# GpSimd's copy in place of a casting transfer for the high half of an expert's weights

## What is computed

```python
logits = einsum('ed,btd->bte', gate_w, x)
scores = sigmoid(logits) + gate_b
weights, indices = top_k(scores, 4)
weights = weights / weights.sum(-1, keepdims=True)
shared_out = silu(x @ w1_shared) * (x @ w3_shared) @ w2_shared
h1 = einsum('btd,edc->btec', x, w1_routed)      # 16 x 512 x 352
h2 = einsum('btd,edc->btec', x, w3_routed)
h3 = silu(h1 * h2)
experts_out = einsum('btec,ecd->bted', h3, w2_routed)
routed_out = einsum('bted,bte->btd', experts_out, router_probs)
```

## Time and profile before

| | |
|---|---|
| Median of three runs | 990.17 us |
| The profiled execution | 990.58 us, of it 989.0 us span |
| Mean granted TensorE clock | 0.908 of full speed |
| Busy: TensorE, its weight loads | 817.7 us (83%), 694.2 us (70%) |
| Busy: VectorE, ScalarE, GpSimd | 425.3, 297.1, 493.6 us |
| GpSimd's queue: software DMA | 108.74 MB, 40.3% of the DMA engines' time |

### The profile page before, as it was taken

The page is one execution under the profiler, slowest core; times in us unless marked ns, Lnnn a source line. Parts: engine busy times, 40 slices in busy tenths (PEclk is TensorE's granted clock), DMA queues, the critical chain, the costliest instruction groups (busy, mean ns, idle before and its releaser), DMA issues.

```text
span 989.0 us, 16683 instructions
## 1 busy us (share of the span) xinstructions
PE 817.7 (83%) x4484; PEld 694.2 (70%) x4485; DVE 425.3 (43%) x864; ACT 297.1 (30%) x577; POOL 493.6 (50%) x357
## 2 busy tenths in 40 slices
PE   3647658786685787999999999999789999969992
PEld 3334536664573666988988888989679988768881
DVE  5576673674444456333333333333223333323331
ACT  1527246245323211222222223222122222212220
POOL 2853217323817645205066555065681168688772
PEclk9668767986987999999999999999889999989997
DMA  6683725806214425537279887497884588959999
GB/s 238 205 302 117 277 64 182 321 21 251 103 32 146 176 110 185 169 91 239 69 245 268 251 248 249 122 273 238 247 273 153 144 248 237 253 128 210 219 175 261
DMA packets 89258, 191.43 MB, mean 194 GB/s; under 512 B 7536, under 2 KB 26992, under 8 KB 89232
## 3 DMA queue, kind: packets, MB, share of 16 engines
q0 software_dynamic: 44800, 108.74, 40.3%
q1 hardware_dynamic: 33920, 61.13, 18.7%
q10 hardware_dynamic: 10512, 21.23, 5.8%
HBM read 85.43 MB, written 67.76 MB: 155 GB/s over the span
## 4 chain that ended last, share of the span: by engine, by line
PE 60%; POOL 11%; DVE 10%; ACT 7%; issue 7%; ACTq 2%; DMA 0%; DVEq 0%; POOLq 0%; SPq 0%
PE bank L594 33%; PE bank L611 14%; PE bank L602 3%; POOL acc L564 2%; PE bank L831 2%; POOL dispatched L508 2%; PE bank L698 2%; PE bank L716 2%; POOL ring_lo L431 2%; ACTq L1057 1%; DVE xr_lo L1419 1%; PE bank L739 1%; POOL hid L489 1%; POOL wa L480 1%; ACT xr_hi L887 1%
## 5 line engine op out<-in xcount | busy, mean ns | idle before, releaser
L594 PE MATMUL bank<-ring_hi,xr_hi 128*128 x632 | 170.1, 351 | 31.9 <-DVE xr_lo L1419 31.6
L594 PE MATMUL bank<-ring_lo,xr_hi 128*128 x632 | 155.5, 328 | 0.0
L594 PE MATMUL bank<-ring_hi,xr_lo 128*128 x632 | 155.4, 327 | 0.0
L594 PEld LDWEIGHTS bank<-ring_hi,xr_hi 128*128 128x128 f32 x632 | 107.0, 192 | 57.4 <-issue 57.3
L431 POOL TENSOR_TENSOR ring_lo<-raw,ring_hi 128x1408 fp32r<-128x1408 f32 x34 | 109.2, 3211 | 59.5 <-DMA ring_hi<-raw 59.2
L887 ACT ACTIVATE ht_hi<-bank 128x384 fp32r<-128x384 f32 x95 | 46.7, 492 | 270.0 <-PE bank L602 270.0
L611 PE MATMUL bank<-ring_hi,ht_hi 112*128 (+3 forms) x285 | 121.7, 427 | 5.8 <-DVE acc L1212 4.5
L1428 DVE TENSOR_TENSOR ht_lo<-bank,ht_hi 128x384 fp32r<-128x384 f32 x79 | 44.0, 557 | 177.6 <-ACT ht_hi L887 177.6
L611 PE MATMUL bank<-ring_lo,ht_hi 112*128 (+3 forms) x285 | 113.3, 398 | 0.0
L594 PEld LDWEIGHTS bank<-ring_hi,xr_lo 128*128 128x128 f32 x632 | 113.0, 191 | 0.0
L594 PEld LDWEIGHTS bank<-ring_lo,xr_hi 128*128 128x128 f32 x632 | 113.0, 191 | 0.0
(11 more groups left out here) (183 smaller groups left out, 1329.5 us busy)
## 6 DMA issues: line engine op xcount, KB each, us to landing
ring_hi<-raw POOLq DMA_DIRECT2D x34, 704.0 KB, 6.0
raw<-in_L_ffn_w_routed_dram POOLq DMA_DIRECT2D x32, 704.0 KB, 6.1
x_in<-dispatched SPq DMA_DIRECT2D x79, 264.0 KB, 4.0
expert_out<-zero_rows ACTq DMA_DIRECT2D x9, 2304.0 KB, 13.5
expert_out<-y_out SPq DMA_DIRECT2D x79, 256.0 KB, 4.3
ring_hi<-raw POOLq DMA_DIRECT2D x17, 768.0 KB, 4.5
raw<-in_L_ffn_w_routed_dram POOLq DMA_DIRECT2D x16, 448.0 KB, 4.6
dispatched<-zero_rows SPq DMA_DIRECT2D x1, 4224.0 KB, 15.9
```

Of the source, the lines that this page charges most:

```text
L594: last = mm(outs[m], half[:, c * P:(c + 1) * P], ring13(w, slot_at, c, m), start=(c == 0 and half is x_hi and w is ring13_hi), stop=(c == ...
```

## The change

`fill` no longer issues transfers for the high halves. GpSimd copies the raw weights into the `float32r` tile itself (`tensor_copy`), waits for its own copy, subtracts, and loads the next raw part at once; then the other weight in the same way, then W2. The semaphores `hi1_in`, `hi3_in`, `hi2_in`, which counted 16 for a transfer, become `hi1`, `hi3`, `hi2`, which count 1 for an instruction. `split_hidden` goes. The wait `free2` now stands behind W3's subtraction. Nothing else is changed.

```diff
-            "raw1_in raw3_in raw2_in hi1_in hi3_in hi2_in ready1 ready3 ready2 "
+            "raw1_in raw3_in raw2_in hi1 hi3 hi2 ready1 ready3 ready2 "
...
-            def split_hidden(n, slot, m):
-
-                hi, lo = (ring[:, slot * W13:(slot + 1) * W13].rearrange(
-                    "p (c m h) -> p c m h", c=KC, m=2)[:, :, m, :]
-                    for ring in (ring13_hi, ring13_lo))
-                pool.wait_ge(s[("hi1_in", "hi3_in")[m]], 16 * n + 16)
-                g.tensor_tensor(lo, raw13[:, :, m, :], hi.bitcast(F32),
-                                ALU.subtract).then_inc(s[("ready1", "ready3")[m]], 1)
-
...
                 free13()
                 wait_alone()
                 for m in range(2):
+                    hi, lo = (ring[:, slot * W13:(slot + 1) * W13].rearrange(
+                        "p (c m h) -> p c m h", c=KC, m=2)[:, :, m, :]
+                        for ring in (ring13_hi, ring13_lo))
+                    rounded, ready = (("hi1", "ready1"), ("hi3", "ready3"))[m]
                     pool.wait_ge(s[("raw1_in", "raw3_in")[m]], 16 * n + 16)
                     wait_alone()
-                    pool.dma_start(ring13_hi[:, slot * W13:(slot + 1) * W13].rearrange(
-                        "p (c m h) -> p c m h", c=KC, m=2)[:, :, m, :],
-                        raw13[:, :, m, :]).then_inc(s[("hi1_in", "hi3_in")[m]], 16)
-                split_hidden(n, slot, 0)
+                    g.tensor_copy(hi, raw13[:, :, m, :]).then_inc(s[rounded], 1)
+                    pool.wait_ge(s[rounded], n + 1)
+                    g.tensor_tensor(lo, raw13[:, :, m, :], hi.bitcast(F32),
+                                    ALU.subtract).then_inc(s[ready], 1)
+                    pool.wait_ge(s[ready], n + 1)
+                    wait_alone()
+                    load_next((1, 3)[m])
                 pool.wait_ge(s["raw2_in"], 32 * n + 32)
                 free2()
                 wait_alone()
-                pool.dma_start(ring2_hi[:, at2:at2 + W2], raw_2).then_inc(s["hi2_in"], 16)
-                split_hidden(n, slot, 1)
-                pool.wait_ge(s["ready1"], n + 1)
-                wait_alone()
-                load_next(1)
-                pool.wait_ge(s["ready3"], n + 1)
-                wait_alone()
-                load_next(3)
-                pool.wait_ge(s["hi2_in"], 16 * n + 16)
+                g.tensor_copy(ring2_hi[:, at2:at2 + W2], raw_2).then_inc(s["hi2"], 1)
+                pool.wait_ge(s["hi2"], n + 1)
```

## The result

| | before | after |
|---|---|---|
| Median (four runs each, 986.36 to 993.12 and 972.52 to 976.69) | 989.76 us | 974.5 us |
| The profiled execution, and its span | 990.58, 989.0 us | 972.52, 969.9 us |
| TensorE's waits for the tokens' low halves | 31.6 us in 26 | 16.2 us in 15 |
| GpSimd busy | 493.6 us | 531.0 us |
| GpSimd's queue: software DMA | 108.74 MB, 40.3% | 70.86 MB, 27.9% |

The ratio is 0.9846 (95% interval 0.9807 to 0.9886): 15.3 us faster, where 984 (977 to 992) was forecast. The direction and the places were right, the size was not: some two and a half times the gain came.

The account below looks back on a forecast made before the run. It took TensorE as the bound, stalled late by GpSimd's fills 11, 12 and 16. Terms −7.5 (these fills), +2.3 (fill 0), −0.9 (fill 2) and −0.4 (DMA relief) made −6.5, hence 984 us, range 977 to 992.

Parts of the forecast that it names:

- The copy and the fill: On GpSimd a copy takes 1.40 us for 1,408 elements, 1.50 for 1,536, and a whole fill 19.26 us.
- Fills 11 and 12: Two late weight fills behind TensorE's stalls at 701 and 721 us: 2.4 us gained over both.
- so it moves with TensorE, to 824.6: The gathers before fill 16 start on a store's landing that follows TensorE, so 824.6 for 827.00; 7.5 us gained altogether.
- So no clock loss is spared: At the last stall, fill 16 still misses ScalarE's wish by 4.1 us, and slower matmuls still follow the idle time.
- Most of the 22 small waits fall late, beside gathers, and stay; I take −0.4: TensorE's small waits, some 10 us together, gain only 0.4 us from 51 fewer transfers, with −4 as the end.
- Fill 2: Near 385 us, VectorE's cast ends sooner, −0.9 us; +3.7 if it meets GpSimd's second subtraction, −3.3 if everything slips between.
- Fill 0: In the first stretch, GpSimd's first subtraction holds up VectorE's small `q_scale` until 34.6 us: +2.3 us on the chain.
- Each microsecond on the copy costs 8: Each us on a copy costs 8 us: five at fill 12, two more at fill 16, one at fill 0.
- Rival 3: Faster: fill 2's cast comes free, small waits shorten, fill 0's delay is absorbed: near 977.5 us, chance 0.20.
- Rival 2: A copy as long as the subtraction, 3.2 us, makes fills 11, 12 and 16 later: 1006 us, chance 0.08.
- rival 1: First form: a copy of 2.1 us; second: 1.4 us with fill 2's cast caught: 990 us either way, chance 0.26.
- Rival 4: TensorE never waits for the transfers, so replacing them by copies changes nothing: 990 us, chance 0.04.

Follow-up runs that it names:

- the square of medians: Kernel before and changed kernel, each with register loads late (989.76, 974.5 us) or moved ahead of a wait (974.3, 965.55 us).
- experiment 4: Changed kernel with fill 0 alone done by transfers, as before: 972.07 us, ratio 0.9806 to the kernel before.
- Experiment 5: Changed kernel with each copy made twice, one behind the other: 1006.93 us, ratio 1.0170 to the kernel before.
- experiment 1: Changed kernel plus casting transfers of the old sizes between dead tiles beside fills 3 to 16: 996.48 us, ratio 1.0066 to the kernel before.

## Why the prediction was wrong, step by step

**The copy and the fill: right.** 34 copies took 1.38 us in the mean, W2's 1.48; I had 1.40 and 1.50. The hop, the load behind a subtraction and the whole fill came as worked out (19.15 for 19.26 us).
```profile
L441 POOL CAST ring_hi<-raw 128x1408 fp32r<-128x1408 f32 x34 | 47.0, 1382 | 165.7 <-PE bank L585 158.5
```
The Trainium skill's GPSIMD Engine Reference, section "Elementwise — side-by-side cycle accounting", would give, as estimates from its figures, 1.21 us by the one and 2.11 by the other; the row lies between, nearer the first.

**Fills 11 and 12: right**, -2.96 for -2.4 us.

**"so it moves with TensorE, to 824.6" failed.** This is the step on the gathers ahead of fill 16. I took the releaser in the earlier trace rows, the landing of a store, for the one that decides. The gathers started at 814.45 us, with the same 1.24 us of idle and no store named; GpSimd's own work is over 1.24 us before, in both kernels:
```profile
812.63 0.58 POOL L415 DMA_DIRECT2D raw<-in_L_ffn_w_routed_dram  x1
814.45 1.68 POOL L555 DMA_INDIRECT acc<-expert_out,out_row  x1 [1.24 <-issue]
...
843.38 1.96 POOL L441 CAST ring_hi<-raw 128x1408 fp32r<-128x1408 f32 x1
845.43 3.22 POOL L443 TENSOR_TENSOR ring_lo<-raw,ring_hi 128x1408 fp32r<-128x1408 f32 x1
...
850.29 3.21 POOL L443 TENSOR_TENSOR ring_lo<-raw,ring_hi 128x1408 fp32r<-128x1408 f32 x1
```
From the start of fill 14 on GpSimd is its own bound in the changed kernel: fill 14, fill 15, 16 gathers, fill 16, with no wait for TensorE over 0.3 us. (Before, one of 1.90 us at 792.88, for the old W2 slot, stood ahead of W3's subtraction in fill 14.) So every fill in the row counts. Fill 14 to fill 15 went from 20.67 to 19.46 us, fill 15 to the gathers from 22.70 to 20.27, the gathers to W3 from 44.62 to 39.05. I had priced the last alone, at 5.1, and it gave 5.6. Fill 15 was longer than my 19.87 for a reason that the trace of before showed, in its second transfer's issue and its first subtraction:
```profile
805.81 0.75 POOL L446 DMA_DIRECT2D ring_hi<-raw  x1 [0.76 <-DMA raw<-in_L_ffn_w_routed_dram]
811.92 3.23 POOL L431 TENSOR_TENSOR ring_lo<-raw,ring_hi 128x1408 fp32r<-128x1408 f32 x1 [5.36 <-DMA ring_hi<-raw]
```
GpSimd waited 5.36 us for its first transfer, where in fill 14 it was 2.62, and 0.76 us for raw weights before the second. Hence the last stall left 0.96 us, not the forecast 3.5. "So no clock loss is spared" fell with it: over the 4 us after the resumption the granted clock was 0.64 before (873.25) and is 1.00 now (855.14).

**"Most of the 22 small waits fall late, beside gathers, and stay; I take −0.4" failed.** The first half held: 14 of the 22 lay from 799 us on, 5.3 us in sum, and 10 of them, 3.3 us, are there still. What failed is the term of 0.4 us, which priced the seven between fills 3 and 11 at next to nothing. Each was a slow register load (3.2 us of waits in sum), and all went: -4.84 us in that stretch, which the idle transfers brought back, and some 6.5 us in all by the square of medians. My own other end was -4. In the chain by line, L1057 and "issue" stood at 2.7% and 2.6% of a stretch in which I looked only for waits of TensorE by releaser.

**Fill 2: the sign was wrong**, +2.19 for -0.9 us. The case "the cast meets the second subtraction" came, priced at +3.7. I had set GpSimd's start at 385.55 us as in the kernel before, 0.16 us before ScalarE's copy for tile 0. It started 1.81 us before that copy (381.71 and 383.52); why in the kernel before the transfer was issued only 0.55 us after TensorE's first transpose of tile 0, while the copy begins 1.09 us ahead of it, no run tells.

**Fill 0: the mechanism was right, its weight in the sum is not shown.** 2.04 us up to the transposes, forecast +2.3; but taking the lock away again (experiment 4) left nothing of them at 176 us. The stretch as a whole got 2.20 shorter, through the clock at 199 to 209 us and an earlier start that lies within the scatter of the traces.

**"Each microsecond on the copy costs 8" failed.** Experiment 5 measured 22 for each us on a copy. The rule counted the fills that were late before; it left out fills 14 and 15 ahead of the gathers and the fills that become late once a copy is longer (542 and 835 us).

**The rivals.** Rival 3 (977.5 us) had the size best, by one right part (the small waits, -3 to -4) and one wrong (the cast free). Rival 2 and the first form of rival 1 fell with the copy's 1.38 us. The second form of rival 1 had its condition come true (the cast of fill 2 was caught) and not its 990 us, for that loss was small beside the two terms above. Rival 4 fell with the stalls, which shrank. With the three failed terms at what they measured (-9.20 for -5.1, -4.84 for -0.4, +2.19 for -0.9) the sum would have read -6.5-4.1-4.4+3.1=-11.9. The other 7.2 us of the 19.10 are 4.5 in the first stretch, mostly scatter and clock, and 2.7 of small terms (-0.6, -1.1, -1.0).

## What to carry to other kernels

When an engine's queue holds several bodies of work in a row with no long wait between them, every body that gets shorter counts, up to the next wait: follow the engine's own timeline back to its last long idle time, and trust a named releaser only if the idle time would be shorter without it. Read the chain by line for stretches without stalls too; a share under "issue" or under an engine's queue is a place where less traffic or an earlier load pays. Register loads belong ahead of the wait in front of them, which here gained as much as the change itself (15.5 us). And after each gain look again at who ends last: here it became the gathers.

## What the runs showed of the hardware

- A register load from SBUF takes 0.27 us at best. At its late place, between fills 3 and 11, the slowest took 1.30 us with casting transfers, 0.30 without them and 1.10 with idle ones; at the early place, without them, 0.41 to 0.55 us. It counts as busy on no engine.
- GpSimd's rounding copy of 128x1408 takes 1.38 us, of 128x1536 1.48 us; one behind the last gather's issue took 1.96 us. Two rows suggest that it holds VectorE too: with each copy made twice, `q_scale` began at 32.76 us and ended at 33.23 instead of after 0.17, as the second copy ended (31.84+1.36=33.20); and the subtraction at 388.72 us of the changed kernel took 0.49 us for 0.23, beside a copy that ended at 389.12. No experiment tested it alone.
- Less traffic shortens other transfers: the tiles' loads (264 KB) landed in 2.8 us for 4.0, the tiles' stores in 2.8 for 4.3, raw weights (704 KB) in 4.9 for 6.1 (medians). With the idle transfers of experiment 1 they took 4.0, 4.2 and 5.5 us again.
- In the first stretch nearly the same work took 2.1 us longer where the granted clock was 0.76 and not 1.00 (199 to 209 us), and 4.9 us longer where it was 0.78 and not 1.00 (340 to 360). What sets it there no run shows.
